# Projecting two query tiles by seven block products instead of eight in a float32 transformer block on one NeuronCore

## The reference

```python
x = x + 0.5 * ffn(layernorm(x))
x = x + attention(layernorm(x))
x = x + 0.5 * ffn(layernorm(x))
```

```python
q, k, v = x @ Wq.T, x @ Wk.T, x @ Wv.T            # per head
q, k = rmsnorm(q, q_norm_w), rmsnorm(k, k_norm_w)
scores = q @ k.T / sqrt(128) + bias               # causal, with ALiBi slopes
out = softmax(scores) @ v
y = concat_heads(out) @ Wo.T
```

## Time and profile before

| | |
|---|---|
| median of 3 runs | 1262.6 us (1262.48 to 1263.76) |
| profiled execution: its time / its span | 1262.72 / 1261.4 us |
| attention, PE's slots 0 to 63 | 268.6 to 1042.5 us |
| length of a PE slot by t = 0, 1, 2, 3 | 12.0, 10.5 (10.9 for n % 8 = 1), 12.3, 14.0 us |
| busy: PE, DVE, ACT, POOL | 98%, 64%, 58%, 42% of the span |
| chain that ended last | PE 85%, ACT 5%, DVE 5%, POOL 2% |
| granted TensorE clock | full in all slices |
| DMA | 60.2 MB, mean 48 GB/s; a tile of 256 KB lands 2.0 us (to y) to 5.5 us (from x) after its issue |

### The profile page before, as it was taken

The page is one execution under the profiler, slowest core; times in us unless marked ns, Lnnn a source line. Parts: engine busy times, 40 slices in busy tenths (PEclk is TensorE's granted clock), DMA queues, the critical chain, the costliest instruction groups (busy, mean ns, idle before and its releaser), DMA issues.

```text
span 1261.4 us, 18366 instructions
## 1 busy us (share of the span) xinstructions
PE 1239.9 (98%) x6562; PEld 1057.1 (84%) x6562; DVE 802.9 (64%) x1978; ACT 733.5 (58%) x1738; POOL 523.8 (42%) x412
## 2 busy tenths in 40 slices
PE   6999999999999999999999999999999989999999
PEld 5788888888888888888888888888888878888887
DVE  7976665766665666666566565666666777655554
ACT  4554443267667657667666666666666684544432
POOL 4686551644225224324315314313413243765550
PEclk9999999999999999999999999999999999999999
DMA  6153222101001001001101001001101010121101
GB/s 227 39 160 114 103 102 84 51 1 56 29 1 50 35 1 51 34 1 51 35 1 51 35 1 51 34 1 51 35 1 51 1 50 1 51 83 51 51 17 67
DMA packets 15018, 60.20 MB, mean 48 GB/s; under 512 B 2064, under 2 KB 2736, under 8 KB 12880
## 3 DMA queue, kind: packets, MB, share of 16 engines
q1 hardware_dynamic: 14688, 58.73, 13.4%
q10 hardware_dynamic: 240, 0.30, 0.1%
HBM read 45.91 MB, written 13.11 MB: 47 GB/s over the span
## 4 chain that ended last, share of the span: by engine, by line
PE 85%; ACT 5%; DVE 5%; POOL 2%; issue 1%; DMA 1%; SPq 0%; DVEq 0%; ACTq 0%; POOLq 0%
PE bank L284 19%; PE bank L285 19%; PE bank L286 19%; PE bank L507 5%; PE bank L363 4%; PE bank L369 4%; PE bank L364 4%; PE bank L518 3%; PE bank L519 3%; PE bank L523 3%; ACT prob L822 2%; PE bank L486 2%; ACT prob L831 2%; POOL o_l L1294 1%; DVE probT_l L1206 1%
## 5 line engine op out<-in xcount | busy, mean ns | idle before, releaser
L1369 POOL TENSOR_TENSOR rows<-rows,row_root_y 128x640 f32<-128x640 f32 x64 | 80.6, 1260 | 271.4 <-DVE row_root_y L926 271.4
L822 ACT ACTIVATE prob<-prob,neg_top 128x128 f32<-128x128 f32 (+3 forms) x256 | 141.5, 555 | 75.7 <-DVE neg_top L1195 75.2
L1363 POOL TENSOR_TENSOR square<-rows 128x640 f32<-128x640 f32 x64 | 80.3, 1255 | 203.1 <-ACT rows L801 203.1
L837 ACT CAST probT_h<-bank 128x512 fp32r<-128x512 f32 x160 | 84.7, 596 | 135.9 <-PE bank L507 135.9
L831 ACT ACTIVATE prob<-prob,inverse 128x128 f32<-128x128 f32 (+3 forms) x256 | 123.4, 557 | 1.8 <-DVE inverse L1200 1.8
L284 PE MATMUL bank<-w_h_late,xnT_hi 128*128 128x512 f32 (+1 forms) x352 | 121.2, 344 | 0.0
L286 PE MATMUL bank<-w_h_late,xnT_lo 128*128 128x512 f32 (+1 forms) x352 | 118.6, 337 | 0.0
L285 PE MATMUL bank<-w_l_late,xnT_hi 128*128 128x512 f32 (+1 forms) x352 | 118.3, 336 | 0.0
L1294 POOL TENSOR_TENSOR w_l_late<-raw_late,w_h_late 128x512 fp32r<-128x512 f32 (+1 forms) x58 | 88.3, 1540 | 68.3 <-ACT w_h_late L615 68.3
L1206 DVE TENSOR_TENSOR probT_l<-bank,probT_h 128x512 fp32r<-128x512 f32 x160 | 101.6, 685 | 21.9 <-ACT probT_h L837 21.8
L1195 DVE CUSTOM_DVE_ANT_0 prob<-bank,bias 128x128 f32<-128x128 f32 (+3 forms) x256 | 109.7, 485 | 0.0
(11 more groups left out here) (181 smaller groups left out, 3465.7 us busy)
## 6 DMA issues: line engine op xcount, KB each, us to landing
raw_late<-w_qkv SPq DMA_DIRECT2D x8, 1536.0 KB, 6.2
raw_early<-ffn_w SPq DMA_DIRECT2D x21, 512.0 KB, 4.2
scaled<-raw_early SPq DMA_DIRECT2D x21, 512.0 KB, 2.6
raw_late<-scaled SPq DMA_DIRECT2D x21, 512.0 KB, 3.6
raw_late<-w_o SPq DMA_DIRECT2D x8, 1024.0 KB, 4.8
y<-x_rows SPq DMA_DIRECT2D x8, 256.0 KB, 2.0
x_rows<-x SPq DMA_DIRECT2D x7, 256.0 KB, 5.5
fac_raw_gu<-ffn_fac SPq DMA_DIRECT2D x13, 32.0 KB, 3.6
```

The source lines that it names most:

```text
L822: last = act.activation(p, p, ACT.Exp, bias=neg_top[:, h:h + 1], scale=-1.0, accum_out=total[:, h:h + 1])
L837: act.copy(probT_h[:, j, :, :], banks[r.bank][:, :].rearrange("p (h q) -> p h q", h=G)).then_inc(probT_hi_done, 1)
L1363: pool.tensor_tensor(square[:, n % 2, :, :], row, row, ALU.mult).then_inc(squares_done, 1)
L1369: pool.tensor_tensor(row, row, by, ALU.mult).then_inc(rows_normed, 1)
```

## The change

**Products.** From group 2 on (`SEVEN_FROM`), two neighbouring query tiles (n, n+1) are projected together. Their tokens are a 2 x 2 block matrix (a11, a12 the two channel halves of tile n, a21, a22 those of n+1), a group's weights another (b11 .. b22: channel halves by column halves of HALF = 384 of the 768 columns). Seven products with sums of blocks (the Winograd form that the feed-forward stages use already) give the four blocks; each is 6 matmuls of 384 columns. The token sums s1 to s4 are made once for the four pairs (slots 4 to 8), the weight differences t1 to t4 for each group. Products 1, 6, 7 and 4 add up in PSUM bank 0; after each ACT copies the bank to `rows` (`take_sum`, `take_left`), and DVE adds products 2, 5 and 3 from other banks (`add_products`). Groups 0 and 1 are projected by two halves of 384 columns.

**Room.** The token sums stand where `x_rows` stood: between the stages the tiles go to DRAM (`x_between`), and `project_out` adds to a tile of a ring of two in SBUF (`x_ring`), which SP loads and stores in each slot.

**Order.** New on PE, ACT, DVE, POOL and SP:

```diff
 # PE: slot
+                ahead = n + LEAD
+                first, second = paired(ahead) and n % 2 == 0, paired(ahead) and n % 2 == 1
+                if ahead == FIRST_PAIRED:
+                    rotation[0] = range(1, BANKS)
                 scores(n)
                 if n:
                     weigh_values(n - 1)
-                if n + LEAD < UNITS:
-                    project(n + LEAD, "q")
+                if first:
+                    product_qkv(ahead, 1)
+                    product_qkv(ahead, 2)
+                elif second:
+                    product_qkv(ahead - 1, 5)
+                    product_qkv(ahead - 1, 7)
+                elif ahead < UNITS:
+                    project(ahead, "left")
                 if n + 1 < UNITS:
                     turn_rows(n + 1)
-                if n + LEAD < UNITS:
-                    project(n + LEAD, "kv")
+                if ahead < FIRST_PAIRED:
+                    project(ahead, "right")
...
                     project_out(n - 1)
+                if first:
+                    product_qkv(ahead, 6)
+                elif second:
+                    product_qkv(ahead - 1, 4)
+                    product_qkv(ahead - 1, 3)
                 turn_probabilities(n)
 # ACT: slot
-                soon = G if unit(n)[2] == 0 or n + LEAD < UNITS else G // 2 if unit(n)[2] == 1 else G - 1
+                soon = G // 2 if unit(n)[2] == 1 else G if unit(n)[2] == 0 or n + LEAD < UNITS else G - 1
                 exponentials(n, range(soon))
                 if n:
                     weigh_values(n - 1)
                 exponentials(n, range(soon, G))
                 probabilities(n)
-                if at == 1:
-                    split_o(g, (2, 3))
...
+                if n % 2 == 0 and paired(n + 2):
+                    values_hi(n + 2)
...
+                if g < HKV - 1:
+                    split_qkv(g + 1, *QKV_WHEN[g + 1 >= SEVEN_FROM].get(at, ()))
+                if 0 <= n - LEAD - 1 < PAIRS:
+                    token_sums_round(n - LEAD - 1)
+                if at == 0:
+                    split_o(g, (0, 1))
+                if paired(ahead):
+                    take_sum(ahead, 6) if n % 2 == 0 else take_left(ahead - 1)
...
                 turn_probabilities(n)
...
                 if at == 0:
-                    split_o(g, (0, 1))
+                    split_o(g, (2, 3))
 # DVE: slot
                 scores(n)
-                if n + LEAD - 1 < UNITS:
-                    sum_squares(n + LEAD - 1)
+                if ahead - 1 < FIRST_PAIRED:
+                    sum_squares(ahead - 1)
...
+                if n == UNITS - LEAD:
+                    turn_rows(n + 1)
+                if n % 2 == 0 and paired(n + 2):
+                    sum_squares(n + 2)
+                    sum_squares(n + 3)
                 if n % 2 == 0 and n + LEAD - 2 < UNITS:
                     pair_roots(n + LEAD - 2)
...
+                if paired(ahead):
+                    add_products(ahead, 2) if n % 2 == 0 else add_products(ahead - 1, 5)
-                if n + 1 < UNITS:
+                if n + 1 < UNITS and n != UNITS - LEAD:
                     turn_rows(n + 1)
...
                     project_out(n - 1)
+                if paired(ahead) and n % 2:
+                    add_products(ahead - 1, 3)
                 turn_probabilities(n)
 # POOL: slot
+                if n % 2 == 0 and paired(n + 2):
+                    square_rows(n + 2)
+                    square_rows(n + 3)
+                mixes_now = QKV_MIX_WHEN.get(at, ()) if SEVEN_FROM <= g + 1 < HKV else ()
+                if at == 4:
+                    mix_qkv(g + 1, *mixes_now)
                 if n + 2 < UNITS:
                     norm_rows(n + 2)
+                if n % 2 == 0 and paired(n + 2):
+                    values_lo(n + 2)
...
+                if at == 3:
+                    mix_qkv(g + 1, *mixes_now)
+                if g < HKV - 1:
+                    split_qkv(g + 1, *QKV_WHEN[g + 1 >= SEVEN_FROM].get(at, ()))
```

More of the change, by code:

```diff
@@ new lines, in take_sum, with take_left @@
+            def take_sum(n, m):
+                r = results["seven", n, m]
+                act.wait_ge(full[r.bank], r.nth)
+                heads = slice(0, LEFT_HEADS) if m == 1 else slice(LEFT_HEADS, G + 2)
+                act.copy(rows[:, (n + (m == 7)) % LEAD, heads, :],
+                         banks[r.bank][:, 0:HALF].rearrange("p (h d) -> p h d", h=LEFT_HEADS)).then_inc(evac[r.bank], 1)
+            def take_left(n):
+                r = results["seven", n, 4]
+                act.wait_ge(full[r.bank], r.nth)
+                act.copy(rows[:, (n + 1) % LEAD, 0:LEFT_HEADS, :],
+                         banks[r.bank][:, 0:HALF].rearrange("p (h d) -> p h d", h=LEFT_HEADS)).then_inc(evac[r.bank], 1)
@@ L804, in turn_rows, with values_hi @@
+            def values_hi(n):
+                for u, m in ((n, 3), (n + 1, 5)):
+                    _, b, t = unit(u)
+                    r = results["seven", n, m]
+                    act.wait_ge(evac[r.bank], r.nth)
+                    act.copy(v_h[:, b, t, :], rows[:, u % LEAD, G + 1, :]).then_inc(v_hi_done, 1)
             def turn_rows(n):
@@ L1353, in split_o, with token_sums_rest, values_lo @@
+            def token_sums_rest(u):
+                pool.wait_ge(token_sums_hi, u + 1)
+                rest(token_sums[u][2][:, :, :], token_sums[u][0][:, :, :], token_sums[u][1][:, :, :]).then_inc(token_sums_lo, 1)
+            def values_lo(n):
+                for u in (n, n + 1):
+                    _, b, t = unit(u)
+                    pool.wait_ge(v_hi_done, u + 1)
+                    rest(v_l[:, b, t, :], rows[:, u % LEAD, G + 1, :], v_h[:, b, t, :]).then_inc(v_lo_done, 1)
             def split_o(g, chunks):
@@ L1512, in load_qkv, with keep_rows, ring_store, ring_load @@
                     sp.wait_ge(full[r.bank], r.nth)
[L1513 removed]
+                sp.dma_start(late_room[0][:, :], w_qkv[g]).then_inc(w_in["qkv"], 16)
+            def keep_rows(b):
+                for t in range(TB):
+                    r = results["down", 0, STEPS - 1, b, t]
+                    sp.wait_ge(evac[r.bank], r.nth)
+                    sp.dma_start(x_between[b * TB + t], xr[b * TB + t][:, :]).then_inc(x_kept, 16)
+                if b == B - 1:
+                    sp.wait_ge(x_kept, 16 * B * TB)
+            def ring_store(n):
+                g, b, t = unit(n)
+                r = results["out", n]
+                sp.wait_ge(evac[r.bank], r.nth)
+                if g < HKV - 1:
+                    sp.dma_start(x_between[b * TB + t], x_ring[:, n % 2, :]).then_inc(ring_out[n % 2], 16)
+            def ring_load(n):
+                g, b, t = unit(n)
+                if n > 1 and unit(n - 2)[0] < HKV - 1:
+                    sp.wait_ge(ring_out[n % 2], 16 * (n // 2))
+                sp.dma_start(x_ring[:, n % 2, :], x_between[b * TB + t]).then_inc(ring_in[n % 2], 16)
             def load_o(g):
[L1516 removed]
+                sp.wait_ge(qkv_lo, sum(len(blocks) for blocks in QKV_BLOCKS[:g + 1]))
                 sp.dma_start(late_room[0][:, 0:G * DM], w_o[g]).then_inc(w_in["o"], 16)
```

334 lines of the change are left out of this document (236 added, 98 removed).

## The result

After the change the kernel takes 1256.2 us (median of 5 runs, 1255.42 to 1256.61), before it 1262.69 (5 runs, 1262.48 to 1263.76): ratio 0.9946, 95% interval 0.9931 to 0.996. It is faster, as forecast, but by 6.5 us instead of 16.8. The forecast was 1245.9; the time lies at the slow end of the range.

A forecast was written before the change was run, and what follows sets the result against it. PE's columns were taken to bound attention (busy 97.83 of 98.00 us in a group). Terms -25.4 - 3.1 + 8.0 + 3.7 = -16.8 us gave 1245.9 us from 1262.7; forecast 1241 to 1250 (0.55), range 1237 to 1257.

The forecast's parts named there:

- PE's saving: Even slots, 24 pairs from unit 16 to 63: three products replace a projection, 1.06 us each, 25.4 us less.
- The wait for `oT_l`: Twelve t = 1 slots (13, 17, ... 57): shorter cover makes PE wait 0.67 us each, 8.0 us more.
- The wait for w_o: PE's wait for POOL's `o_l` goes, since w_o's last hi parts come earlier: seven groups, 0.44 each, 3.1 us less.
- DVE's even slots at nothing: Even slots: DVE's added sums and addition of product 2 still finish 0.2 us before PE's next slot; no cost.
- The end of attention: Slots 60 to 63: two sums and the roots stand ahead of slot 61's `probT_l` and scores; 3.7 us more.
- The rest at nothing: POOL's added work (13 us a group), ACT's three more weight copies and the tile's DRAM trips stay covered; no cost.
- All the saving arrives: Rival: `oT_l` is ready in t = 1 slots, so the 8.0 us wait is absent; 1237.9 us, chance 0.10.
- spill in even slots: Rival: small unseen costs miss DVE's or t = 2's margin, 0.3 us in each of 24 slots; 1253.1 us, chance 0.17.
- POOL beside the roots: Rival: late t4 on POOL holds a root instruction on DVE in six groups, +10 us; 1255.9 us, chance 0.10.
- the slower one: Rival: in even slots the addition of product 2 waits for ACT's copy; 1269.9 us at 1 us a slot, chance 0.08.
- The DMA's trips: One tile load and one store a slot, 2 to 5.5 us each, two slots ahead of use; counted at nothing.

The follow-up runs named there:

- e4_split_last: Changed kernel with ScalarE's splits of w_qkv and its differences moved behind the turned probabilities in every slot; 1263.9 us.
- e5_wo_as_before: Changed kernel with ScalarE's splits of w_o put back where they stood before the change, behind the turned probabilities; 1272.51 us.
- e2_roots_ahead: Changed kernel with slot 60's two sums of squares ahead of the weighed values and its roots ahead of unit 61's turned rows; 1250.59 us.
- e3_values_first: Changed kernel with VectorE's rest of the weighed values (oT_l) ahead of the reciprocal in t = 1 slots from slot 5 on; 1248.22 us.
- e6_margin: Changed kernel with three unread 10-column products of two SBUF inputs added behind the roots in VectorE's 24 even slots; 1287.97 us.

## Why the prediction was wrong, point by point

Of the 11.2 us between the sums of forecast and slots, slot 12 is 5.9, PE's saving 2.4, slot 61 with its neighbours 1.9, slots 0 to 11 1.3, and the slots with t = 1 give 0.3 back.

**PE's saving: right mechanism, 2.4 us too large.** Even slots gave 0.97 to 1.01 us instead of 1.06, and t = 3 slots took 0.07 back. A group of twelve matmuls of 384 columns takes 2.08 to 2.11 us in the slots, where 2.08 was counted, and the group behind the transposes 0.1 more (the output projection now stands there and takes 2.85 us for 2.75, where the narrower projection had carried it). The products alone were counted; the change of neighbours was not.

**The wait for `oT_l`: right.** 8.0 us forecast, 0.67 a slot; the experiment that takes it away made the 12 slots 7.3 us shorter, 0.61 each. In slots with n % 8 = 1 it took the place of the wait for w_o at the same row. The step held, and it said that the cover was short; it didn't ask whether DVE's order could make it long enough.

**The wait for w_o: right in place.** No `o_l` wait is left from slot 9 to 57. It gave 6 x 0.44 us, not 7, because slot 9 lost as much at its head, and slot 1 lost 0.49: in both ACT's split of w_o stands ahead of the turned probabilities, and the first matmul on these waits for `probT_h`. With the splits put back, the slots with t = 1 lose 14.7 us.

**DVE's even slots at nothing: right**, and the margin of 0.2 us too; the experiments put it at 0.16 to 0.2.

**The end of attention: right in its 3.7 us, wrong in calling that the price.** It was paid in full on DVE, but the time showed 5.6: the wait was long enough for the granted clock to fall, and the sum had costed every wait at the full clock.

**"The rest at nothing": this is the step that failed.** The term was put at nothing for the whole kernel. It counted POOL's idle time (66 of 98 us) and ACT's, and asked of the differences only whether they are ready when PE multiplies with them. It didn't look at what stands ahead of them on POOL, and what stands behind their splits on ACT, at the one change from unpaired to paired groups: squares that wait for ACT, the differences behind them, ACT's split behind these, the turned probabilities behind the split. The runs show 5.9 us in one slot, 3.1 of waiting and 2.8 at the lower clock, and moving the differences ahead of the squares took all of it away. That question was asked of the even slots, which repeat 24 times, and not of slot 11, which occurs once. The count itself was short as well, at no cost in time: 3.5 us of POOL's work in a group are eight rests of the values (`v_l`), which run there now and aren't in the prediction's 13 us.

**The rivals.** "All the saving arrives" fell, as did "spill in even slots", "POOL beside the roots" (its time, 1255.9, was met by luck, from other causes: in the paired groups no root row is longer than 0.17 us) and the slower one: in even slots the addition of product 2 follows the roots without idle time; DVE waits for ACT's copy in odd slots alone (1.6 and 2.1 us). The DMA's trips stayed hidden: a 256 KB load lands in 2.6 us in the median.

What remains open: why the same wait of 1.95 us is followed by the lower clock in slots 21, 37 and 53 of e4_split_last and not in 29 and 45, and the same waits for `o_l` in slot 17 of e5_wo_as_before and not in its five kin. Slot 12's excess, too, was 5.9, 5.7 and 4.8 us (the changed kernel, e2_roots_ahead, e3_values_first), though these kernels don't differ there.

## What to carry to other kernels

Idle time of an engine is no cover for a step that is put behind a waiting instruction: follow the order of each queue through the one place where the pattern changes (first pair, last slots), since steady slots show nothing of it. When a cover is shortened, look at once for a row on the next engine that only stands in the way, as the reciprocal did for 8 us. And cost an idle TensorE of 1.5 us and more at up to twice its length: here 3.1 us of waiting came to 5.9, and 1.97 to 3.4.

## What the runs showed of the hardware

- Behind PE waits of 3.1 us the granted clock fell to 0.50 (1.2 GHz) for 417 to 420 us and was full again by 423: 1.7 to 2.8 us on top of the wait. Two waits of 1.6 us behind each other did it too, waits of 1.33 to 1.40 us alone did not (23 of them in e6_margin), one of 1.95 to 1.97 did in three slots out of five, and waits of 0.37, 1.36 and 0.26 us within 5 us in one slot out of six.
- Three VectorE instructions of 10 columns beside POOL's norm of the rows took 1.78 us where 0.62 was expected, with one SBUF input (product with a constant) as with two; sums of the same columns took 0.16 us each, beside POOL or not. In this kernel that is a difference of 29 us.
